# A block of two mixture-of-experts layers around attention: the attention weights are loaded and split at the end of the first expert stage, and VectorE normalises the first six attention tiles

## The reference

```python
x = x + 0.5 * ffn(layernorm(x))
x = x + attn(layernorm(x))
x = x + 0.5 * ffn(layernorm(x))

def ffn(h):        # 32 experts, 6 per token, at most 192 tokens per expert, plus one shared expert
    scores = sqrt(softplus(h @ gate_w.T))
    topk_idx = top_k(scores + bias, 6)
    w = 1.5 * scores[topk_idx] / sum(scores[topk_idx])
    g, u = xb @ w_gate[e], xb @ w_up[e]            # xb: the tokens of expert e, width 512 -> 256
    y[e] = (silu(g) * u) @ w_down[e]               # 256 -> 512
    return sum_over_chosen(w * y) + (clip(silu(h@sg.T) * (h@su.T), -10, 10) @ sd.T)

def attn(h):       # 4 query heads, 1 key/value head of width 128, causal, within each sequence of 1024
    q, k, v = h @ wq, h @ wk, h @ wv
    q, k = rope(rmsnorm(q) * gq), rope(rmsnorm(k) * gk)
    return (softmax(causal(q @ k.T * 128**-0.5)) @ v) @ wo
```

## Time and profile before

| what | us |
|---|---|
| the three executions | 1617.62, 1611.74, 1614.36 |
| median | 1614.36 |
| the profiled execution, own time | 1612.06 |
| span of the profiled execution, first to last instruction | 1609.9 |
| first expert loop: first gather issued, end of the block | 209.7, 514.1 |
| attention: first load, first SP load issued for it | 514.1 |
| last softmax normalisation on POOL | 1098.0 |
| second expert loop: first gather issued | 1313.6 |

### The profile page before, as it was taken

How to read it: one execution, slowest core, us unless ns; L and a number is a source line. 1 busy time by engine, 2 the same in 40 slices (tenths; PEclk the granted TensorE clock), 3 DMA queues, 4 the chain that set the end, 5 groups by cost and what they waited for, 6 DMA issues and landing times.

```text
span 1609.9 us, 23872 instructions
## 1 busy us (share of the span) xinstructions
PE 1467.6 (91%) x8436; PEld 1228.2 (76%) x8436; DVE 1106.0 (69%) x2094; ACT 1027.1 (64%) x2046; POOL 775.6 (48%) x655
## 2 busy tenths in 40 slices
PE   5999989998992889999999999988999989999986
PEld 4877778888882768887887888766787768887875
DVE  5659868776871466766666677665658968877864
ACT  6861558876882467666667666665863438877864
POOL 0114245657654666656556655521113234567664
PEclk9999999999997799999999999999999999999998
DMA  8736479999975101111111121022864559999994
GB/s 281 248 119 207 119 268 330 265 276 263 292 194 94 47 27 40 40 49 58 39 41 53 40 92 53 33 71 67 282 202 148 149 167 312 287 271 264 298 248 64
DMA packets 113492, 257.59 MB, mean 160 GB/s; under 512 B 21248, under 2 KB 22208, under 8 KB 113120
## 3 DMA queue, kind: packets, MB, share of 16 engines
q1 hardware_dynamic: 90848, 204.16, 38.8%
q0 software_dynamic: 22528, 51.92, 15.6%
HBM read 187.27 MB, written 68.76 MB: 159 GB/s over the span
## 4 chain that ended last, share of the span: by engine, by line
PE 37%; DMA 12%; POOL 6%; DVE 5%; issue 4%; ACT 3%; DVEq 1%; POOLq 0%; SPq 0%; ACTq 0%
DMA out<-e_y,slots 11%; PE a_bank L91 4%; PE a_bank L93 4%; PE a_bank L92 4%; POOL out L953 4%; PE a_bank L1643 3%; PE a_wide L1634 2%; PE a_wide L1631 2%; PE a_wide L1635 2%; PE a_bank_o L91 2%; PE a_bank_o L93 2%; PE a_bank_o L92 2%; POOL e_xg L946 1%; DVEq L1458 1%; PE a_bank L1610 1%
## 5 line engine op out<-in xcount | busy, mean ns | idle before, releaser
L1044 DVE TENSOR_TENSOR e_w_lo<-e_raw,e_w_hi 128x1024 fp32r<-128x1024 f32 x192 | 234.2, 1220 | 29.7 <-ACT e_w_hi L979 29.7
L1567 POOL TENSOR_SCALAR t_prob<-t_prob,t_inv 128x128 f32<-128x128 f32 (+7 forms) x128 | 112.0, 875 | 223.4 <-DVE t_inv L1465 223.2
L979 ACT ACTIVATE e_w_hi<-e_raw 128x1024 fp32r<-128x1024 f32 x192 | 202.2, 1054 | 0.0
L946 POOL DMA_INDIRECT e_xg<-htab,slots x128 | 153.0, 1195 | 72.8 <-issue 34.4
L1118 PE MATMUL e_ps_gate<-e_xt,e_w_hi 128*128 128x384 f32 x512 | 164.0, 383 | 0.0
L1118 PE MATMUL e_ps_up<-e_xt,e_w_hi 128*128 128x384 f32 x512 | 150.9, 360 | 0.0
L424 POOL TENSOR_SCALAR d_inter<-d_inter 128x512 f32<-128x512 f32 x32 | 26.5, 827 | 254.4 <-DVE d_inter L557 254.2
L953 POOL DMA_INDIRECT x_after_ffn<-e_y,slots x64 | 101.9, 1592 | 90.2 <-DMA x_after_ffn<-e_y,slots 79.3
L953 POOL DMA_INDIRECT out<-e_y,slots x64 | 103.1, 1610 | 84.3 <-DMA out<-e_y,slots 73.6
L1352 ACT ACTIVATE t_prob<-a_wide,t_neg_max,a_q_scale 128x128 f32<-128x128 f32 (+7 forms) x128 | 106.5, 832 | 55.4 <-DVE t_neg_max L1459 55.1
L1119 PE MATMUL e_ps_gate<-e_xt,e_w_lo 128*128 128x192 f32 x512 | 132.5, 259 | 0.0
(11 more groups left out here) (223 smaller groups left out, 4451.7 us busy)
## 6 DMA issues: line engine op xcount, KB each, us to landing
e_raw<-in_w_experts SPq DMA_DIRECT2D x192, 512.0 KB, 6.3
htab<-d_h SPq DMA_DIRECT2D x16, 1024.0 KB, 5.2
d_x<-in_x SPq DMA_DIRECT2D x16, 512.0 KB, 7.0
d_xs<-in_x SPq DMA_DIRECT2D x32, 256.0 KB, 3.4
x_after_ffn<-d_xs SPq DMA_DIRECT2D x32, 256.0 KB, 3.3
q_x<-x_after_ffn SPq DMA_DIRECT2D x32, 256.0 KB, 3.0
t_res<-x_after_ffn SPq DMA_DIRECT2D x32, 256.0 KB, 2.6
x_after_attention<-t_res SPq DMA_DIRECT2D x32, 256.0 KB, 2.0
```

What stands on the lines that cost most here:

```text
L946: pool.indirect_dma_start(xg[e % GATHERED][q][:, :], None, htab, row).then_inc(gathered[e % GATHERED], 16)
L979: act.activation(third(w_hi[e % 2], c), third(raw[e % 3], c), ACT.Copy).then_inc(hi_ready, 1)
L1044: dve.tensor_tensor(third(w_lo[e % 2], c), third(raw[e % 3], c), third(w_hi[e % 2], c).bitcast(F32), ALU.subtract).then_inc(lo_ready, 1)
L1567: pool.tensor_scalar(prob[:, u, 0:width(i)], prob[:, u, 0:width(i)], inv[:, u:u + 1], 1.0, ALU.mult, ALU.mult).then_inc(p_ready, 1)
```

## The change

Two things are changed.

- The ten chunks leave the expert loop. Behind the last weight third of the last expert SP loads the attention weights in five parts of 128 x 1024 (512 KB each), into the places in SBUF where the low parts will stand (`wqkv_raw`, `wo_raw` lie at the same addresses as `wqkv_lo`, `wo_lo`). Behind its last `weigh`, ACT waits for all five loads and writes the five high parts; DVE subtracts in place. SP no longer waits for `y_stored` of the front's buffers, nor for `att_split`.
- The norm of the tiles 0 to 5 goes from POOL to DVE, in the same slots. On DVE it stands in front of the other pieces of the slot (`add_rotated`, `scale_k`, `turn_q`). The tiles 6 to 31 stay on POOL.

```diff
@@ allocate_kept
+            if part == "lo":
+                raw_w = nc.alloc_sbuf_tensor_at(f"{name}_raw", shape, F32, offset=at)
+                k.wqkv_raw, k.wo_raw = (raw_w, None) if name == "wqkv" else (k.wqkv_raw, raw_w)
@@ routed_experts, SP
-            for c in range(min(XS, len(attention_chunks))):
-                sp.wait_ge(y_stored[c], 16 * ((NT - 1 - c) // XS + 1))
-                load_chunk(c)
             for e in range(E - 3):
                 for c in range(3):
                     sp.wait_ge(lo_ready, 3 * e + c + 1)
                     load_weights(e + 3, c)
-                if XS <= e + XS - 2 < len(attention_chunks):
-                    sp.wait_ge(att_split, e - 1)
-                    load_chunk(e + XS - 2)
+            for hi, lo, raw_w, from_ in attention_parts:
+                sp.dma_start(raw_w, from_).then_inc(att_loaded, 16)
@@ routed_experts, ACT
                 if ahead:
                     split(e + 1, 2)
-                if 0 <= e - 1 < len(attention_chunks):
-                    split_chunk(e - 1)
             weigh(E - 1)
+            if n == 0:
+                act.wait_ge(att_loaded, 16 * len(attention_parts))
+            for hi, lo, raw_w, from_ in attention_parts:
+                act.activation(hi, raw_w, ACT.Copy).then_inc(att_hi, 1)
@@ routed_experts, DVE
-                if 0 <= e - 1 < len(attention_chunks):
-                    split_chunk(e - 1)
+            for c, (hi, lo, raw_w, from_) in enumerate(attention_parts):
+                dve.wait_ge(att_hi, c + 1)
+                dve.tensor_tensor(lo, raw_w, hi.bitcast(F32), ALU.subtract)
@@ attention, DVE
+            def normalise_x(T):
+                dve.wait_ge(rstd_ready, T // 2 + 1)
+                if T >= 2:
+                    dve.wait_ge(t_ready, T - 1)
+                w = T // 2 % 2
+                dve.tensor_scalar(h[T % 2][:, :], x[T % 2][:, :], mv[w][:, T % 2, 0:1], rstd[w][:, T % 2:T % 2 + 1],
+                                  ALU.subtract, ALU.mult).then_inc(h_ready, 1)
...
                     for u in range(2):
+                        if (C := due(T, m, NORM_AT[u], u)) is not None and C < LEAD:
+                            normalise_x(C)
                         if (C := due(T, m, ROT_AT[u], u)) is not None:
                             add_rotated(C)
@@ attention, POOL
-                        if (C := due(T, m, NORM_AT[u], u)) is not None:
+                        if (C := due(T, m, NORM_AT[u], u)) is not None and C >= LEAD:
                             normalise_x(C)
```

More of the change, by code:

```diff
@@ L906, in routed_experts @@
         turned = lambda c: ps_t[c][:, 0:TC].rearrange("p (k s) -> p k s", k=2)
-        attention_chunks = []
+        attention_parts = []
         if n == 0:
-            att_loaded, att_hi, att_split = ([sem(f"e_att_loaded{u}_") for u in range(XS)], sem("e_att_hi"),
-                                              sem("e_att_split"))
-            cut = lambda ap, c: ap.rearrange("p k c -> p (k c)")[:, c * D:(c + 1) * D]
-            attention_chunks = [tuple(cut(ap, c) for ap in (hi[:, :, :], lo[:, :, :], from_))
-                                for hi, lo, from_, size in ((k.wqkv_hi, k.wqkv_lo, a["w_qkv"], WQKV),
-                                                            (k.wo_hi, k.wo_lo, a["w_out"], H * D))
-                                for c in range(size // D)]
+            att_loaded, att_hi = sem("e_att_loaded"), sem("e_att_hi")
+            cut = lambda ap, c: ap.rearrange("p k c -> p (k c)")[:, c * THIRD:(c + 1) * THIRD]
+            attention_parts = [tuple(cut(ap, c) for ap in (hi[:, :, :], lo[:, :, :], raw_w[:, :, :], from_))
+                               for hi, lo, raw_w, from_, size in ((k.wqkv_hi, k.wqkv_lo, k.wqkv_raw, a["w_qkv"], WQKV),
+                                                                  (k.wo_hi, k.wo_lo, k.wo_raw, a["w_out"], H * D))
+                               for c in range(size // THIRD)]
         @block.sync
@@ L921, in load_weights @@
                 sp.dma_start(third(raw[e % 3], c), third(a["w_experts"][e, :, :], c)).then_inc(w_loaded[e % 3][c], 16)
-            def load_chunk(c):
-                sp.dma_start(xs[c % XS][:, :], attention_chunks[c][2]).then_inc(att_loaded[c % XS], 16)
             sp.wait_ge(done.dense, FB * G)
@@ L1009, in weigh @@
                                    scale=xg[e % GATHERED][q][:, D + e:D + e + 1]).then_inc(y_ready, 1)
-            def split_chunk(c):
-                hi, lo, from_ = attention_chunks[c]
-                act.wait_ge(att_loaded[c % XS], 16 * (c // XS) + 16)
-                act.activation(hi, xs[c % XS][:, :], ACT.Copy).then_inc(att_hi, 1)
             act.wait_ge(done.dense, FB * G)
@@ L1070, in split_inner @@
                                   ALU.subtract).then_inc(ilo_ready, 1)
-            def split_chunk(c):
-                hi, lo, from_ = attention_chunks[c]
-                dve.wait_ge(att_hi, c + 1)
-                dve.tensor_tensor(lo, xs[c % XS][:, :], hi.bitcast(F32), ALU.subtract).then_inc(att_split, 1)
             split(0, 0)
```

## The result

The changed kernel takes 1607.37 us (median of 20 runs, 1593.41 to 1619.27), the one before, on the same chip, 1614.34 (20 runs, 1606.35 to 1622.32). The ratio is 0.9947 with an interval of 0.9926 to 0.9967. The forecast was 1611.6 with 1604.5 to 1618 as its range, and "no change" as the likeliest of the three outcomes. Two later series gave ratios of 0.997 (0.9933 to 1.0008) and 0.9934 (0.9896 to 0.9971).

The account below looks back on a forecast made before the run. The prediction took the landings of POOL's scatters to pace the first expert loop. -4.3 + 3.2 + 0.8 there and -2.0 at the attention's start gave -2.3 from 1613.95: 1611.6 us, range 1604.5 to 1618.

Parts of the forecast that it names:

- Taking the chunks out: First expert loop, scatters of experts 0 to 5: without chunks as fast as the second loop, -4.3 us.
- the upper bound, -6.7: First expert loop without chunks: the most it could gain, the two loops' difference over all 31 periods.
- The tail loads: Behind the last expert's weights: five loads keep the queue full and slow 1.4 scatter periods, +3.2 us.
- Experts 24 to 27: Sign of the tail loads' cost: these experts' first scatters over 27 us apart, against 24.37 before.
- The split: End of the first loop: work mostly hidden, but one scatter issue beside it gets longer, +0.8 us.
- The attention's start: Norms of tiles 0 to 5 on DVE: earlier projections -2.6, tile 4's norm +0.6, together -2.0 us.
- The 21.4: Sign in the attention's start: PE's projection of tile 2 at 21.4 us after the first load, against 24.7.
- Tile 4's norm in front of `scale_k`: Attention's start on DVE: one more instruction before the pair PE waits for, +0.6 us; sign, near 1 us long.
- Rival 2: Attention's start: PE's stretch at the lower clock goes too, giving -5.7 in all, 1608.3 us; chance 0.10.
- rival 1: End of the first loop: the tail loads cost nothing, -7.9 in all, 1606.0 us; chance 0.25.
- Rival 3: Scatters of experts 25 to 30: the tail costs more than the chunks did, +5.9, 1619.9 us; chance 0.12.
- Rival 4: Attention's start: norms no faster on DVE because POOL holds it up, -0.3 in all, 1613.6 us; chance 0.08.

Follow-up runs that it names:

- ramp_only: The kernel before with only the norms of tiles 0 to 5 moved from POOL to DVE; 1607.58 us, ratio 1.0001.
- chunks_no_loads: The kernel before without its ten chunk loads, copies and subtractions kept, so the attention computes with other weights; 1602.37 us, ratio 0.9945.
- no_loads: The changed kernel without the attention weights' five loads, splits kept on the last experts' weights; 1604.62 us, ratio 0.9983.
- late_wqkv: wo_in_attention with the input projection's three parts issued only after expert 30's scatters land, ACT waiting for each part by itself; 1599.55 us, ratio 0.9923.
- after_again: The changed kernel, unchanged, run again against the kernel before; 1603.77 us, ratio 0.997.
- after_third: The changed kernel, unchanged, run a third time against the kernel before; 1607.6 us, ratio 0.9934.
- weights_only: The changed kernel with the norms of tiles 0 to 5 back on POOL; 1610.48 us, ratio to the kernel before 1.0007.
- four_norms: The changed kernel with the norms of tiles 4 and 5 back on POOL; 1609.16 us, ratio to the kernel before 0.9975.
- before_again: The kernel before, unchanged, run once more; 1612.12 us, ratio 1.0011.
- no_dve_split: The changed kernel with ACT writing zeros as low parts in place of DVE's five subtractions; 1604.19 us, ratio to the kernel before 0.9958.
- wo_four_norms: wo_in_attention with the norms of tiles 4 and 5 back on POOL; 1601.51 us, ratio to the kernel before 0.9954.
- wo_in_attention: The changed kernel with the output projection's two parts loaded and split in the attention's start; 1604.11 us, ratio to the kernel before 0.9951.

## Why the prediction was right, and where its sizes were off

Each step of the sum was found in the traces, with its sign and near its size, and none of the rivals was. The time, 1607.37, lies inside the range, 4.2 us under the forecast. That it does is in part luck. The medians differ by 7.0 us where the sum had 2.3, and the steps as measured explain 3.7. Of the outcomes the prediction held "no change" likelier (0.48) than "faster" (0.37), with 1609.5 as the limit, and the kernel came out faster.

**Taking the chunks out: -4.3 forecast, -6.5 found.** With the chunk loads experts 0 to 5 take 50.94 on the mean of three executions, without them 44.47 on the mean of the ten executions that have neither the loads nor the chunks. This is the term that was most mis-sized. The measure was right, the second loop, but I took it from one execution, 46.90, and this is the highest of 14: they lie between 42.48 and 46.90, with a mean of 44.81. With that mean the same step gives -6.4 from the trace of before, or -6.1 from the mean of three. That the upper bound, -6.7 over all 31 periods, holds is luck: the 31 periods of the second loop vary by 19 us from execution to execution. Between experts 5 and 24 the kernels with chunk loads took 165.5 on the mean and those without 165.8, so on the mean nothing is won or given back there.

**The tail loads: +3.2 forecast, +4.2 found.** Experts 25 to 27 take 18.55 on the mean of the six kernels with all five parts, against 14.31 on the mean of the six that load nothing there (the two runs of before, ramp_only, chunks_no_loads, no_loads, late_wqkv). The step counted 1.4 slow periods at 2.25 more each; the first was 3.1 longer and the second 1.1. Experts 24 to 27, for which the prediction asked over 27 us, took 26.4 to 28.4 in the six, and in two of them less than 27. Of the total, 2.9 us hang on the three parts of the input projection alone (the two kernels with only these, 17.19).

**The split: +0.8 forecast, +1.0 found.** Periods 29 to 31 take 14.41 on the mean of the six kernels whose subtractions meet an issue (after, after_again, after_third, weights_only, no_loads, four_norms), and 13.38 on the mean of before, before_again, ramp_only, chunks_no_loads, no_dve_split and late_wqkv. (`wo_four_norms`, with three subtractions that meet an issue, took 14.03.) It isn't always one issue of 2.22: in three of the six two issues are long, such as 2.25 and 1.96. Taking DVE's part away made both issues 1.42 again, so the cause is DVE's subtractions. Why they lengthen an issue no run shows. The Trainium skill (SBUF — State Buffer, section "SBUF: two separate sides") has a rule near it: a VectorE instruction with two SBUF inputs and a GpSimd instruction that reads SBUF exclude each other for a whole instruction. A whole subtraction of 1.2 us for each of the two issues, +2.4, was not seen here: the longest issue beside the split, in `four_norms`, took 2.40, one 1.0 more, and the longest pair, in `no_loads`, 2.25 and 1.96, took 1.4 more.

**The attention's start: -2.0 forecast, -2.4 found.** The mean of the four executions with norms on POOL is 797.58, that of the seven with six norms on DVE (no_loads aside) 795.16. (With `no_loads` taken in, the difference is 2.7.) The first exponential moves from 43.08 to 40.62, -2.5. Of the parts, on the mean of the same executions: the projection of tile 0 starts at 8.21 and not 10.04 after the first load, 1.8 earlier and not 2.1 (a norm of 0.50, not 0.46, is a small part of that), that of tile 2 at 22.54 and not 25.14, 2.6 as forecast. This agreement is in part luck. In the 9 us from 8 us after the first load on, which hold most of tile 0's projection, the granted clock isn't the same from execution to execution, and tile 2 follows it: with norms on POOL it starts at 24.53 where that clock was 0.78, and at 25.84 where it was 0.60; with norms on DVE at 22.27 with 0.79 and at 23.07 with 0.67. At like clock (24.53 with 0.78 in `before_again`, 22.31 with 0.77 in `after_third`) the gain is 2.2. The 21.4 that the prediction named as a sign leaves out the 0.6 that its own sum takes off; with it the sign would have been 22.0. ACT's squares of tile 0 end at 21.20 after the first load (538.16 - 516.96) where they ended at 22.04 before (536.12 - 514.08), 0.8 earlier and not 2.1: tile 0's projection starts 1.7 earlier but reaches ACT's `q_raw` 10.81 after its start and not 9.84, which is 1.0 more where the sum had put 0.6 for the clock. Tile 4's norm in front of `scale_k` costs 0.5 against 0.6, but it took 0.54 and not the near 1 us that the prediction wanted to see.

Rival 2 wanted the clock's low stretch to go. One window of 34 us, from 8 us after the first load on, in the kernel before and in the changed one (us; busy us of PE, PEld, DVE, ACT, POOL; granted clock, DMA share, GB/s):

```profile
522.08:556.08 34.00, 26.61 (x131) 22.68 (x130) 14.02 (x29) 13.86 (x53) 22.41 (x18) 0.80 0.14 37
```

```profile
524.96:558.96 34.00, 27.86 (x134) 23.76 (x134) 16.73 (x34) 15.14 (x56) 15.24 (x15) 0.80 0.19 55
```

The granted clock is 0.80 in both, and in the same window of all the other executions, so the rival doesn't hold: no time at the lower of the two levels (1.2 and 2.4 GHz) went. From 531.08 to 550.08 it was 0.82 before and 0.91 in the same place after, but `weights_only`, whose norms are on POOL, shows 0.91 there as well.

**The rivals.** The tail loads cost 4.2, so rival 1 (they cost nothing) is wrong, though its time, 1606.0, is nearer to the result than the forecast. Rival 3 (the tail costs more than the chunks) needed 5 us more at the tail than at the front; it is 5.2 against 6.5 the other way. Rival 4 (norms no faster) is refuted by norms of 0.50 to 1.52, against 2.07 on POOL, and by the earlier start.

**The sum.** -6.5 + 4.2 + 1.0 - 2.4 = -3.7 us, against -2.3 forecast. The ratios say -8.6, -4.8 and -10.7 (of 1614.34, 1610.05 and 1615.11); only the interval of the second holds -3.7. The medians say -7.0, -6.3 and -7.5. So some 3 us of the gain (1 to 7 by the ratios) are in no stretch that the change touches. The two profiled executions of before have spans of 1609.9 and 1612.1, the three of the changed kernel 1610.5, 1599.0 and 1603.2; the means differ by 6.8, and 3.2 of these lie in the second loop, 264.59 against 261.41, which both kernels run alike. The periods between experts 5 and 24 (161.8 to 171.0) and the second loop vary by more than that from execution to execution, with and without the change, and 14 profiles don't settle it. This stays open. So does the choice among the versions: the intervals of `late_wqkv` and `wo_in_attention` overlap those of the changed kernel.

## What to carry to other kernels

Loads that share the DMA engines with a chain of scatters cost the chain time at both of the places tried: moving 2.6 MB from the first expert steps to the last ones exchanged 6.5 us for 4.2, and putting part of it beside the last scatter only turned the wait into one for the split. When a term is the difference between two loops of one trace, first see how far the same loop varies from one execution to the next: here one reading of 46.90 was 2.1 us above the mean of 14, half of the term. And where profiled executions of two kernels agree while their medians don't, compare stretch by stretch over several executions before saying where the time went.

## What the runs showed of the hardware that was not expected

- fp32 TENSOR_TENSOR instructions of 128x1024 on DVE, five back to back, lengthened both indirect scatter issues beside them, from 1.42 to 2.25 and 1.96 us (`no_loads`); ACT's activations of the same size, ten in a row, left them at 1.42 (`no_dve_split`).
- DVE's norm of 128x512 took 0.50 to 0.54 us, 1.52 when POOL's 128x640 multiplication ran beside it, and 0.91 beside POOL's next ones.
- The expert loop that the change doesn't touch took between 250.73 and 270.18 us from one execution to the next.
- Over 34 us, from 8 us after the attention's first load on, the clock was granted at 0.80 whether the norms stood on POOL or on DVE, while in the first 9 of them it lay anywhere between 0.60 and 0.83.
